# A perceiver block on one core: first keys loaded and projected in two halves, lead-in turns in another order

## What is computed

```python
x = x + xattn(layernorm(x), ctx, ctx)        # x: (2, 256, 256), ctx: (2, 4096, 256)
# in it, with q = layernorm(x):
qh   = (q @ w_q).reshape(B, L, 16, 16)
kvp  = c @ w_kv                              # 16 columns of k, 16 of v, shared by the heads
k, v = kvp[..., :16], kvp[..., 16:]
prob = softmax(einsum('bhid,bjd->bhij', qh, k) / 4)
out  = einsum('bhij,bjd->bhid', prob, v) @ w_concat
x = x + attn(layernorm(x)); x = x + moe(layernorm(x))   # untouched
```

## Time and profile before

| | us |
|---|---|
| median of three executions | 633.71 (627.20 to 636.61) |
| the profiled execution | 633.59 |
| its span of instructions | 631.8 |
| TensorE busy | 582.3 (92% of the span) |
| VectorE busy | 465.1 (74%) |
| ScalarE busy | 410.4 (65%) |
| GpSimd busy | 118.3 (19%) |

### The profile page before, as it was taken

How to read it: one execution, slowest core, us unless ns; L and a number is a source line. 1 busy time by engine, 2 the same in 40 slices (tenths; PEclk the granted TensorE clock), 3 DMA queues, 4 the chain that set the end, 5 groups by cost and what they waited for, 6 DMA issues and landing times.

```text
span 631.8 us, 11892 instructions
## 1 busy us (share of the span) xinstructions
PE 582.3 (92%) x4512; PEld 322.6 (51%) x4512; DVE 465.1 (74%) x685; ACT 410.4 (65%) x834; POOL 118.3 (19%) x150
## 2 busy tenths in 40 slices
PE   3798999999999999999999998998999987789995
PEld 1363443444444444444444443466766655678885
DVE  6787887887999999899899994625545556584554
ACT  1347887888888887888888788654555540543451
POOL 4000000000000000000000001302355440357873
PEclk9999999999999999999999999899999997898998
DMA  8640001000000000000000000100001000122321
GB/s 316 245 142 1 2 1 32 37 3 1 1 2 2 1 2 1 2 2 1 1 3 1 1 1 2 34 1 1 25 26 43 17 5 5 58 84 75 100 83 34
DMA packets 11381, 21.99 MB, mean 35 GB/s; under 512 B 1858, under 2 KB 6724, under 8 KB 10308
## 3 DMA queue, kind: packets, MB, share of 16 engines
q1 hardware_dynamic: 11332, 21.31, 10.0%
HBM read 20.78 MB, written 0.52 MB: 34 GB/s over the span
## 4 chain that ended last, share of the span: by engine, by line
PE 73%; DVE 15%; ACT 5%; issue 4%; DMA 2%; POOL 1%; SPq 0%; DVEq 0%
PE bank L574 21%; PE bank L585 16%; DVE mxp L1170 11%; PE pairS L838 6%; PE pairS L663 5%; PE bank L855 4%; PE pairS L713 3%; ACT Pb L962 2%; PE bank L738 2%; PE bank L724 2%; PE bank L517 1%; PE pairS L824 1%; PE pairS L568 1%; DMA ctx<-ctxT 1%; PE pairS L593 1%
## 5 line engine op out<-in xcount | busy, mean ns | idle before, releaser
L1170 DVE TENSOR_REDUCE mxp<-pairS 128x1 f32<-128x1024 f32 x256 | 306.7, 1221 | 36.1 <-PE pairS L568 34.9
L962 ACT ACTIVATE Pb<-bank 128x512 f32<-128x512 f32 x512 | 274.0, 599 | 56.4 <-PE bank L574 43.8
L574 PE MATMUL bank<-qparts,kparts 64*128 64x512 f32 x512 | 189.7, 453 | 12.9 <-DVE mxp L1170 6.4
L568 PE MATMUL pairS<-kparts,qparts 64*128 64x512 f32 x512 | 189.3, 455 | 2.8 <-DVE mxp L1170 2.0
L585 PE MATMUL bank<-Pb,V 128*32 128x256 f32 x2048 | 151.6, 389 | 1.2 <-ACT accS L948 1.2
L574 PEld LDWEIGHTS bank<-qparts,kparts 64*128 64x128 f32 x512 | 78.6, 184 | 117.2 <-ACT Pb L962 75.5
L585 PEld LDWEIGHTS bank<-Pb,V 128*32 128x32 f32 x2048 | 46.5, 108 | 74.4 <-issue 47.5
L568 PEld LDWEIGHTS pairS<-kparts,qparts 64*128 64x128 f32 x512 | 78.0, 184 | 7.6 <-DVE mxp L1170 2.5
L383 POOL CAST mparts<-mneg 128x8 fp32r<-128x8 f32 x16 | 3.2, 199 | 368.6 <-DVE mneg L1178 368.6
L1241 DVE TENSOR_REDUCE smx<-pairS 128x2 f32<-128x512 f32 x32 | 21.8, 686 | 32.7 <-PE pairS L713 32.7
L398 POOL TENSOR_TENSOR Pb<-Pb,srd 128x512 f32<-128x512 f32 x32 | 33.3, 1041 | 66.6 <-DVE srd L1246 66.3
(11 more groups left out here) (176 smaller groups left out, 730.5 us busy)
## 6 DMA issues: line engine op xcount, KB each, us to landing
ctx<-ctxT SPq DMA_DIRECT2D x4, 2048.0 KB, 8.4
wU<-w_up SPq DMA_DIRECT2D x18, 256.0 KB, 2.7
wD<-w_down SPq DMA_DIRECT2D x18, 128.0 KB, 2.4
wA<-w_qk SPq DMA_DIRECT2D x8, 256.0 KB, 2.7
wO<-w_out SPq DMA_DIRECT2D x8, 128.0 KB, 2.1
wV<-w_v SPq DMA_DIRECT2D x2, 512.0 KB, 3.7
xs<-x SPq DMA_DIRECT2D x2, 256.0 KB, 6.0
out<-xs SPq DMA_DIRECT2D x2, 256.0 KB, 2.2
```

Of the source, the lines that this page charges most:

```text
L568: last = mm(dst[:, i * 512:(i + 1) * 512], qparts[rows, at:at + P], kparts[c // NCH][rows, k:k + 512], start=True, stop=True)
L574: mm(dst[:], kparts[g // NCH][rows, s * P:(s + 1) * P], qparts[rows, g * CW:(g + 1) * CW], start=True, stop=True).then_inc(exp_filled, 1)
L962: A(PT[:, s % 8, :], src, ACT.Exp, scale=1.0 / np.sqrt(XD)).then_inc(exp_free, 1)
L1170: nc.vector.reduce_max(mxp[:, c % 2 * NBLK + blk, kp:kp + 1], pairS[n % 2][:], AX).then_inc(max_free, 1)
```

## The change

The first half of batch 0's keys is itself cut in two: `("kv", 0, 0, 0)` and `("kv", 0, 0, 1)`, each two groups of 512 keys, each in partitions 0 to 63 or 64 to 127 of its bank and of `kvh` and `kvl`. Each has its own load of 1024 keys and its own turn, ScalarE move and VectorE subtraction. The table puts the first quarter's projection first of all, the query transposes behind it, and the second quarter's projection behind the first two maxima; other turns stand in other places. `wq` and the x of batch 1 are loaded between the two quarters. V's arrays are cleared by GpSimd instead of VectorE. VectorE's layer norm of batch 1 moves from ahead of its walk to just ahead of the table's entry `("qT", 0, 0)`, which lies behind its subtraction for the first quarter. No turn moves between lead-in and main loop: the lead-in still holds 20 maxima.

```diff
-PRO = [("xT", 0), ("kv", 0, 0), ("qT", 0, 0), ("ks", 0, 0), ("ks", 0, 1), ("qs", 0), ("max", 0, 0, 0), ("max", 0, 1, 0),
...
+PRO = [("kv", 0, 0, 0), ("xT", 0), ("ks", 0, 0), ("ks", 0, 1), ("qT", 0, 0), ("qs", 0), ("max", 0, 0, 0),
+       ("max", 0, 1, 0), ("kv", 0, 0, 1), ("max", 0, 2, 0), ("max", 0, 3, 0), ("ks", 0, 2), ("ks", 0, 3), ("max", 0, 0, 1),
...
+def kv_turn(b, t):
+    return ("kv", 0, 0, t // 2) if (b, t // 4) == (0, 0) else ("kv", b, t // 4)
+def kv_rows(what):
+    return slice(64 * what[3], 64 * what[3] + 64) if len(what) == 4 else slice(0, P)
...
-            sp.dma_start(wq[:], w_q.rearrange("(k p) n -> p k n", p=P)).then_inc(wq_in, 16)
+            def load_first(i):
+                keys = slice(i * S // 4, (i + 1) * S // 4)
+                sp.dma_start(ctx[0][:, :, keys], ctxT[0].rearrange("(k p) s -> p k s", p=P)[:, :, keys]
+                             ).then_inc(first_in[i], 16)
...
-            load_ctx(0, 0)
+            load_first(0)
+            sp.dma_start(wq[:], w_q.rearrange("(k p) n -> p k n", p=P)).then_inc(wq_in, 16)
             sp.dma_start(xs[:, 2:4, :], x_dram[:, 2:4, :]).then_inc(x1_in, 16)
+            load_first(1)
             load_ctx(0, 1)
             for s in range(2):
-                sp.wait_ge(exp_filled, EXP_TURN["kv", 0, s] + 1)
+                sp.wait_ge(exp_filled, EXP_TURN[kv_turn(0, 4 * s + 3)] + 1)
                 load_ctx(1, s)
...
+            for b in range(B):                                   # GpSimd
+                nc.gpsimd.memset(V[b][:], 0.0).then_inc(v_init, 1)
+                pool.wait_ge(v_init, 2 * b + 1)
+                nc.gpsimd.memset(V[b][:, :, XD:XD + 1], 1.0).then_inc(v_init, 1)
...
-            def kv_proj(b, s):
-                dst = exp_bank(("kv", b, s))
-                pe.wait_ge(ctx_in[b][s], 16)
-                if b + s == 0:
+            def kv_proj(b, s, part=None):
+                if part is None:
+                    dst, groups = exp_bank(("kv", b, s)), range(4)
+                    pe.wait_ge(ctx_in[b][s], 16)
+                else:
+                    dst, groups = exp_bank(("kv", b, s, part)), (2 * part, 2 * part + 1)
+                    pe.wait_ge(first_in[part], 16)
                     pe.wait_ge(wkv_in, 16)
                 for k in range(KD):
-                    for j in range(4):
+                    for j in groups:
                         last = mm(dst[32 * j:32 * j + 32, :], wkv[:, k, :],
...
-            for b in range(B):                                   # VectorE
-                nc.vector.memset(V[b][:], 0.0).then_inc(v_init, 1)
-                dve.wait_ge(v_init, 2 * b + 1)
-                nc.vector.memset(V[b][:, :, XD:XD + 1], 1.0).then_inc(v_init, 1)
...
-            dve.wait_ge(x1_in, 16)
-            layer_norm(range(2, 4))
             for what in PRO:
+                if what == ("qT", 0, 0):
+                    dve.wait_ge(x1_in, 16)
+                    layer_norm(range(2, 4))
```

More of the change, by code:

```diff
@@ L52 @@
 NPAIR_K = S // 1024
[L53 to L59 removed]
+PRO = [("kv", 0, 0, 0), ("xT", 0), ("ks", 0, 0), ("ks", 0, 1), ("qT", 0, 0), ("qs", 0), ("max", 0, 0, 0),
+       ("max", 0, 1, 0), ("kv", 0, 0, 1), ("max", 0, 2, 0), ("max", 0, 3, 0), ("ks", 0, 2), ("ks", 0, 3), ("max", 0, 0, 1),
+       ("qT", 1, 0), ("max", 0, 1, 1), ("kv", 0, 1), ("max", 0, 2, 1), ("max", 0, 3, 1), ("ks", 0, 4), ("ks", 0, 5),
+       ("max", 0, 0, 2), ("xT", 1), ("max", 0, 1, 2), ("ks", 0, 6), ("ks", 0, 7), ("max", 0, 2, 2), ("qs", 1),
+       ("max", 0, 3, 2), ("qT", 0, 1), ("max", 0, 0, 3), ("v", 0, 0), ("max", 0, 1, 3), ("qs", 2), ("max", 0, 2, 3),
+       ("v", 0, 1), ("max", 0, 3, 3), ("qs", 3), ("max", 1, 0, 0), ("qT", 1, 1), ("max", 1, 0, 1), ("qs", 4),
+       ("max", 1, 0, 2), ("qs", 5), ("max", 1, 0, 3), ("rows", 0)]
 LATER = [("kv", 1, 0), ("qs", 6), ("v", 1, 0), ("ks", 1, 0), ("ks", 1, 1), ("ks", 1, 2), ("ks", 1, 3), ("kv", 1, 1),
@@ L245, in build @@
         ctx_in = [[sem(f"ctx_in{b}{s}") for s in range(2)] for b in range(B)]
+        first_in = [sem(f"first_in{i}") for i in range(2)]
         x1_in = sem("x1_in")
@@ L523, in k_rows @@
                 dst, n, j = exp_bank(("ks", b, t)), 2 * b + t // 4, t % 4
-                have(("kv", b, t // 4))
+                have(kv_turn(b, t))
                 if b + t == 0:
                     pe.wait_ge(pick_done, 1)
-                mm(dst[:], pickK[0][:, j, :], kvh[:, n % 2, :], start=True, stop=False)
-                mm(dst[:], pickK[1][:, j, :], kvl[:, n % 2, :], start=False, stop=True).then_inc(exp_filled, 1)
+                rows = kv_rows(kv_turn(b, t))
+                mm(dst[:], pickK[0][rows, j, :], kvh[rows, n % 2, :], start=True, stop=False)
+                mm(dst[:], pickK[1][rows, j, :], kvl[rows, n % 2, :], start=False, stop=True).then_inc(exp_filled, 1)
             def v_rows_of(b, s):
                 dst, n = exp_bank(("v", b, s)), 2 * b + s
-                have(("kv", b, s))
+                have(kv_turn(b, 4 * s + 3))
                 for t in range(4):
@@ L911, in q_high, with kv_high @@
                 A(qh[:, m, b * L:(b + 1) * L], src[:, 0:L], ACT.Copy).then_inc(exp_free, 1)
-            def kv_high(b, s):
-                src = filled(("kv", b, s))
-                A(kvh[:, (2 * b + s) % 2, :], src, ACT.Copy).then_inc(exp_free, 1)
+            def kv_high(*at):
+                what = ("kv", *at)
+                src, rows = filled(what), kv_rows(what)
+                A(kvh[rows, (2 * at[0] + at[1]) % 2, :], src[rows, :], ACT.Copy).then_inc(exp_free, 1)
             def k_move_rows(b, t):
@@ L1161, in low_part @@
                 else:
-                    i = (2 * what[1] + what[2]) % 2
-                    dst, high, src = kvl[:, i, :], kvh[:, i, :], EXP[n % 3][:]
+                    i, rows = (2 * what[1] + what[2]) % 2, kv_rows(what)
+                    dst, high, src = kvl[rows, i, :], kvh[rows, i, :], EXP[n % 3][rows, :]
                 dve.wait_ge(exp_free, n + 1)
```

6 lines of the change are left out of this document (removed).

## The result

The changed kernel took 639.9 us, the median of four executions (635.08 to 641.6), against 631.95 us (627.2 to 636.61) of the kernel before. The ratio on record, which is not the quotient of these two medians, is 1.0101, with a 95% interval of 1.006 to 1.0143: slower by about 1%, outside the predicted range of 628.5 to 638, though within the 2% that was called no difference. A second batch gave 640.56 against 634.44 us, a ratio of 1.0086 (1.0055 to 1.0116). The profiled execution of the changed kernel was the fastest of its four, 635.08 us with a span of 633.3.

The account below looks back on a forecast made before the run. TensorE was taken to bound the main loop, VectorE the lead-in's maxima. Terms -1.4 + 2.25 - 0.9 = -0.05 us, plus 0.1 for buffer waits, gave 633.6 us (633.7 against the median), no difference; range 628.5 to 638.

Parts of the forecast that it names:

- the load's term: Head of the lead-in: the first quarter of keys takes 2.5 us at 418 GB/s and lands at 6.8, at latest 8.1.
- the waits between the maxima: Lead-in, VectorE between first and last maximum: 3.0 us of waits in 8 places, against 1.69 in 4 before.
- The bound and the passing on: Main loop: TensorE is busy 97%, so any shift of its start passes to the total unchanged.
- rival C: Head of the lead-in: first quarter lands late, each us past 6.8 adding one; at 8.1, +1.3, 634.9 us; chance 0.15.
- The quarter's price: First key projection: a quarter's 8 instructions cost the full 3.64 us of 16, since the rounds stay, half as full.
- Rival A: Key projections: a quarter costs half, by number of products; 2.2 us less, 631.4 us; chance 0.10.
- The layer norm in the chain: VectorE ahead of the first maximum: batch 1's layer norm takes 3.97 us, 11.8 to 15.8, and `ql` waits on it.
- From the first maximum to the end of the last: Lead-in's 20 maxima on VectorE: 28.9 us instead of 26.64, 2.25 us longer, from one more subtraction and more waits.
- The tail: End of the lead-in: `qs` 5 ahead of the last product brings the first score product 0.9 us back, to 46.9.
- rival D: Head of the lead-in: clock rises later than `ks` 0, adding 0.3 to 1.3 us, up to 634.9 us; chance 0.10.
- the head: Lead-in up to the first maximum: it starts at 18.4 instead of 19.81, 1.4 us earlier.

Follow-up runs that it names:

- before_tail: The kernel before with only `qs` 5 moved ahead of the last maximum's product: 634.31 us, ratio 1.0018.
- no_ln: The changed kernel with the second layer norm replaced by a plain copy of x: 637.4 us, ratio 0.9995.
- before_2: The kernel before, same code, profiled a second time: 638.6 us (one execution).
- split_alone: The changed kernel with the table's old order and batch 1's layer norm back ahead of VectorE's walk: 635.65 us, ratio 1.0023.
- ln_merged: The changed kernel with x in one load and one layer norm over both batches ahead of VectorE's walk: 638.25 us, ratio 1.0092.
- after_gaps: The changed kernel with unused TensorE products in the lead-in's gaps, none at the start: 632.42 us, ratio 1.0005.

## Why the prediction was wrong

Two steps failed. One is a term that the forecast put at nothing: that TensorE's clock, once up, could fall again in the lead-in. The other is the load's term, too small by 1.84 us. A third, the waits between the maxima, was slightly too small.

**The bound and the passing on: right for the main loop.** The shift at its start lasted through its 16 chunks, 3.38 to 3.48 us. "Nothing makes that shift smaller or larger later" does not hold behind it: between the same ScalarE instructions of the two profiles it is 4.6 us from 450 to 525 us, 1.7 from 545 on, and 1.4 at the end.

**The load: mis-sized.** I had it land at 6.8 us, with 8.1 as the other end; it landed at 8.64, and at 7.76 to 8.66 in the profiles with this load order and table. The step that failed is "at 418 GB/s it takes 2.5 us". From 3 to 5 us little was moved (windows of 1 us, changed kernel):

```profile
3.00:4.00 1.00, 0.00 (x0) 0.00 (x0) 0.40 (x2) 0.00 (x0) 1.00 (x2) 1.00 0.97 187
4.00:5.00 1.00, 0.00 (x0) 0.00 (x0) 0.90 (x6) 0.00 (x0) 0.94 (x5) 1.00 0.89 274
```

That is not all of it. Only the loads of the two quarters have packets of 4096 bytes, and 0.79 MB of these had started by 6.0 us; the remaining 0.26 MB took until 8.6, and from 6 to 8 us 0.42 MB of the loads behind, in packets of 1024 bytes, were moved as well. Whether these took the quarter's place, or some of the DMA engines were late with their part of it, no run shows; `wq`, next in the queue, landed at 9.25, behind the quarter. This was rival C, and it came with the price that it named: 1.84 us later than forecast, and the first maximum 1.8 later (20.20 for 18.4).

**The quarter's price: right.** Eight instructions took 3.63 us, sixteen 3.64. Rival A, the price by products, is refuted. By the rule of the Trainium skill ("TensorE: Matmul & The Clock Gate", section "Measured speedup vs the span model") halving the tiles of a pack saves nothing, and the trace agrees (3.63 against 3.64 us). The cut across columns, which halves the length of each instruction, is what halves the time.

**The layer norm in the chain: right.** It took 13.54 to 17.49 = 3.95 us (forecast 3.97) and set `ql`. I had not priced that it could be moved out of the chain.

**From the first maximum to the end of the last: 30.43 us for 28.9.** VectorE's waits came in eight places, as forecast, and are 1.53 + 0.39 + 0.25 + 0.97 + 0.51 + 0.21 + 0.22 + 0.21 = 4.29 us for 3.0. The first alone is 1.53 for 0.5: the second quarter's projection, priced at 1.92, took 2.90 and stood behind products that were slow too. With idle work and the clock kept up the stretch is 28.22 + 1.22 = 29.44. So the sum of the waits was short by 0.5 at most (idle work may itself delay a product), and the remaining 1.0 us of this profile goes with the clock.

**The tail: right in the sum, not in its cause.** From the start of the 20th maximum to the first exponential 1.44 us for 2.23, thus 0.8 for the forecast 0.9. But `qs` 5 ahead of the last product gave only 0.45 of it by itself (before_tail).

**The missing term.** The forecast knew that the clock starts low and rises (rival D), and took the granted column of 1.00 ahead of the products as settled from then on. It never asked whether the new order could let it fall again. The new table leaves TensorE idle for 2.05 + 0.69 us between the query projection and the first products, and then for 0.85 to 0.93 us at four places. The profiles with the new table and without idle work (no_ln left out) are at the lower level for 3.4 to 10.2 us, 8.2 in the mean. Each 3.4 us lengthen the stretch of the maxima by 1.0 to 1.5 us (29.21, 31.44 and 32.66 against 28.22): 2.4 stretches, some 3 us.

**The sum again**, by the runs, against a kernel before whose clock holds in the lead-in: the head +0.4 us (19.93 and 20.20 against 19.34 to 19.86, the means), the order's own waits 28.22 - 25.43 = +2.8, the tail -0.8, and the falls about +3: 5.4, where the second batch showed 6.1 in the medians and 5.9 in the means (the first, of four executions each, 8.0 in the medians). The forecast had the first three at -1.4 + 2.25 - 0.9, and the fourth at nothing. This agreement is not proof. The falls' 3 us count in full only if the kernel before seldom falls; before_2 speaks against that, though only 3 of 117 executions of the kernel before took as long as its 638.6 us. And the split by the mean clock leaves 3.7 us to all but the clock, where the marks give 2.4. The two profiled executions differ by only 1.5 us in total (633.59 and 635.08), as later falls lay differently: the kernel before was at the lower level for 10.2 us from 528.6 on, the changed one for 3.4 us from 534.6 on, and it is there that the shift drops from 4.6 to 1.7 us.

What stays open: why the clock falls in one execution of the same code and not in another, and how often it does in the kernel before (two profiles, one with 20.5 us). That idle gaps are the cause rests on the idle work, which removed the falls in the lead-in; how much idle time is needed was not measured: in before_2 the clock fell with no wait of TensorE above 0.88 us in the 7 us ahead of it.

## What to carry to other kernels

Before an order of turns is changed, look at where it leaves TensorE idle, and not only at what bounds a stretch: where VectorE is the bound, TensorE's slack is no free cover, since its clock can fall there and then turn TensorE into the bound. In split_alone and ln_merged a lead of 2.2 and 2.3 us at the first maximum was mostly or wholly gone at the 20th, with 6.8 us at the lower level in between. Cut a packed projection so that each instruction gets shorter, not so that the pack gets emptier. Take several profiles of the same code before a shift of 1 us in a landing, or of a few us in the total, is put down to a change.

## What was not expected of the hardware

- TensorE's granted clock fell in the middle of a lead-in, after it had idled for 2.05 us (changed kernel), and once, with no wait above 0.88 us in the 7 us ahead of it, in a program that had shown no fall in another execution (before_2). It stayed low there for 20.5 us, in which TensorE was busy for 20.42: once low, half speed made it the bound and the first exponential came 8.1 us later.
- The granted column reads 1.00 at the first projection, though this ran at half speed (3.63 us at 7.76, against 1.91 at 19.16, in after_gaps). Lengths of like instructions tell the level at the start, not that column.
- A pack of two column groups took 3.63 and 1.91 us at the two levels, a pack of four with half the columns 1.07 at the higher one.
- A load of 1 MB issued at 1.75 was waited for until 8.64, though the queues moved 351 to 386 GB/s from 5 us on, with the loads behind it among them. With the same loads the wait ended at 7.76 to 8.66 us in five profiles.
